# Attention and experts on one core: max scores in the opening, a repacked memory chain, and a longer lead of the maxima

## The reference

```python
q, k, v = qkv of x, 16 heads of 16                      # per batch
attn = softmax(causal(q @ k.T) * scale);  seq_out = attn @ v
w1, w2 = projections of x, previous position / position  # 16 heads of 4
r1, r2 = projections of x
write_lines = exterior(w1, w2); read_lines = exterior(r1, r2)   # 6 components, each divided by its norm
M[t] = decayed sum over s < t of J w[s] (x) J w[s]       # 6 x 6, per head
rd_M = rd @ M;  mem_score = (1 - a) * sum(rd_M * rd) + a * sum(rd_M * rd_M)
gate = sigmoid(memg)
out = (seq_out + mean over heads of (sigmoid(mem_score * mem_scale) * gate) * mem_val) @ out_w.T + out_b
```

## Time and profile before

| | us |
|---|---|
| median of 3 runs | 914.86 (911.75 to 915.72) |
| the profiled execution | 906.65 |
| its span | 904.9 |

### The profile page before, as it was taken

One profiled execution on the slowest core, in us unless ns is written; L12 is line 12 of the kernel. 1 busy time (PEld: TensorE's weight loads), 2 busy tenths in 40 slices (PEclk: granted clock), 3 DMA queues, 4 the chain that ended last, 5 costly groups with the idle time before them and its releaser, 6 DMA issues.

```text
span 904.9 us, 12625 instructions
## 1 busy us (share of the span) xinstructions
PE 763.1 (84%) x4116; PEld 521.5 (58%) x4116; DVE 623.1 (69%) x2123; ACT 353.3 (39%) x709; POOL 409.7 (45%) x334
## 2 busy tenths in 40 slices
PE   6587664888988989989799895787899999999995
PEld 3343432545654656556556553455788788887874
DVE  2126554866886878868878689973677877777775
ACT  2120422544554544545546452373233332422420
POOL 9100644964654655646445565133324433433420
PEclk9887686989998999999989995578899999999998
DMA  8896368347564564656553732513022023022001
GB/s 290 186 238 116 73 98 136 73 93 147 83 158 92 112 150 68 149 110 108 135 106 72 163 66 43 155 47 93 1 71 94 1 94 94 2 93 93 24 1 47
DMA packets 60423, 89.90 MB, mean 99 GB/s; under 512 B 8235, under 2 KB 37317, under 8 KB 60357
## 3 DMA queue, kind: packets, MB, share of 16 engines
q1 hardware_dynamic: 60356, 89.09, 44.0%
HBM read 54.72 MB, written 33.82 MB: 98 GB/s over the span
## 4 chain that ended last, share of the span: by engine, by line
PE 47%; DVE 25%; DMA 12%; POOL 6%; issue 4%; ACT 3%; SPq 3%; ACTq 0%; POOLq 0%; DVEq 0%
PE ps L1242 19%; DVE ps L466 7%; PE ps L336 7%; PE ps L372 6%; PE ps L325 6%; DMA Q<-MT 6%; DVE Ob L514 5%; PE ps L313 4%; DMA qk_scratch<-HL 2%; PE ps L1208 2%; DMA Wm<-mem_scratch 2%; SPq L677 2%; PE ps L230 1%; ACT X L1228 1%; DVE nmax L466 1%
## 5 line engine op out<-in xcount | busy, mean ns | idle before, releaser
L466 DVE CUSTOM_DVE_ANT_0 ps<-ps,mask 128x256 f32<-128x256 f32 (+3 forms) x512 | 238.4, 510 | 87.0 <-PE ps L313 86.9
L409 ACT ACTIVATE Pr<-ps 128x512 f32<-128x512 f32 (+2 forms) x384 | 189.6, 527 | 152.9 <-PE ps L325 146.6
L325 PE MATMUL ps<-Q,K 98*128 98x256 f32 (+2 forms) x512 | 179.2, 393 | 51.0 <-DMA Q<-MT 40.6
L313 PE MATMUL ps<-K,Q 96*128 96x256 f32 (+2 forms) x512 | 163.5, 365 | 30.0 <-DVE nmax L466 28.8
L652 POOL TENSOR_SCALAR_AFFINE_SELECT Pr<-Pr 128x512 f32<-128x512 f32 x128 | 87.9, 692 | 215.7 <-ACT Pr L409 213.5
L1242 PE MATMUL ps<-ew_hi,XT 128*128 128x512 f32 x512 | 180.7, 415 | 0.0
L325 PEld LDWEIGHTS ps<-Q,K 98*128 98x128 f32 x512 | 97.2, 206 | 136.3 <-ACT Pr L409 54.4
L1368 DVE SCALAR_TENSOR_TENSOR A<-ps,cw,A 128x256 f32<-128x256 f32 x256 | 123.7, 483 | 53.6 <-PE ps L1242 42.0
L313 PEld LDWEIGHTS ps<-K,Q 96*128 96x128 f32 x512 | 105.0, 211 | 50.6 <-DVE nmax L466 42.7
L336 PE MATMUL ps<-Pr,V 128*17 128x512 f32 (+3 forms) x1024 | 107.5, 497 | 8.1 <-POOL Pr L652 8.1
L1242 PEld LDWEIGHTS ps<-ew_hi,XT 128*128 128x128 f32 x512 | 100.8, 197 | 21.4
(11 more groups left out here) (183 smaller groups left out, 1124.4 us busy)
## 6 DMA issues: line engine op xcount, KB each, us to landing
qk_scratch<-HL SPq DMA_DIRECT2D x32, 512.0 KB, 3.2
Q<-qk_scratch SPq DMA_DIRECT2D x96, 128.0 KB, 4.0
K<-qk_scratch SPq DMA_DIRECT2D x96, 128.0 KB, 5.7
Pr<-xT SPq DMA_DIRECT2D x8, 512.0 KB, 9.4
xraw<-xT SPq DMA_DIRECT2D x8, 512.0 KB, 6.2
mem_scratch<-Rl SPq DMA_DIRECT2D x16, 256.0 KB, 5.7
mv_scratch<-MV SPq DMA_DIRECT2D x32, 128.0 KB, 1.7
Wm<-mem_scratch SPq DMA_DIRECT2D x16, 256.0 KB, 10.2
```

The lines of the kernel that those rows point to most:

```text
L313: last = nc.tensor.matmul(o, Q[0:STACK, hh, P * i:P * i + P], K[0:STACK, hh, 0:n], start=True, stop=True)
L325: last = nc.tensor.matmul(o, K[0:STACK + 2, hh, P * kt:P * kt + P], Q[0:STACK + 2, hh, T - n:T], start=True, stop=True)
L409: nc.scalar.activation(probs(g % 2, kt, heads[0], len(heads)), src, ACT.Exp, scale=SCALE).then_inc(s_exp, 1)
L466: last = nc.vector.tensor_tensor_reduce(out=scores, in0=scores, in1=mask[:, T - w:T], scale=1.0, scalar=NEG, op0=ALU.add, op1=ALU.max, acc ...
```

## The change

- `LEAD = 8`: `ahead` uses u+8 instead of u+6, so max scores are 20 units ahead of the exp scores; the turn of the maxima comes at unit 4. After the opening, 8 units of group 1 are issued instead of 6.
- In the opening, each of the steps 4 to 7 is followed by three units of the max scores of group 0 (`scores`). The memory tiles 8 to 15 use two PSUM banks in turn instead of four, since the max scores use the others. The stacks of batch 0 are issued behind projections 3, 4, 5 and 6, and x of batch 1 behind projection 4.
- The loads of Wm are in halves of four batches: the first before the maximum rows of group 0, the second after them. The loads of the read projections are in halves too, in the groups 2 and 3 of batch 0 in SP's program, behind the maximum rows.
- The norms of both kinds of lines are computed on POOL, in five steps each (`norms`); DVE keeps the reciprocals, which lie in groups 0 and 1 of batches 1 and 2.
- The memory chain has 18 slots of one group each, from batch 2 to group 1 of batch 6. Three slots hold two halves: slot 0 outer, slot 1 apply and the next outer, slot 2 its apply. Scans lie in units 6, 8 and 10 of slot 0 and units 0, 2 and 4 of slot 2. POOL's masks are called singly and placed between these steps. The products and sums for the score follow on POOL in groups 2 and 3 of batch 6, and DVE has three score steps, in units 5 to 7 of group 1 in batch 7, instead of thirteen.

```diff
+LEAD = 8
+        def tile_bank(m):
+            return ps[m % 4] if m < 8 else ps[2 + m % 2]
-        def opening(project, memory, fold):
+        def opening(project, memory, fold, scores):
...
                 project(j)
+                scores(3 * (j - 4))
...
-                    pe.wait_ge(s_p1e[m % 2], m // 2 - 1)
+                    pe.wait_ge(s_p1e[m % 2], m // 2 - 1 if m < 8 else m // 2)
...
-            k = g + (1 if u < 6 else 2)
-            return k // NG, k % NG, (u + 6) % UNITS
+            k = g + (1 if u + LEAD < UNITS else 2)
+            return k // NG, k % NG, (u + LEAD) % UNITS
...
-                    if u == 6 and not (last and g == NG - 1):
+                    if u == UNITS - LEAD and not (last and g == NG - 1):
                         pe_turn_max(pe, b + (g + 1) // NG, (g + 1) % NG)
...
-                    if first:
-                        dve_write_norms(dve, UNITS * g + u)
-                    if last:
-                        dve_read_norms(dve, UNITS * g + u)
-                    if scan and (g, u) in SCAN_AT:
-                        dve_scan(dve, b, SCAN_AT.index((g, u)))
-                    if last and 9 <= UNITS * g + u < 22:
-                        dve_score_step(dve, UNITS * g + u - 9)
+                    if b in (1, 2) and g < 2 and u in (4, 10):
+                        dve_inverse(dve, Ob[:, 2, :] if b == 1 else Wm[:, 6, :], 2 * g + u // 10,
+                                    ML_WNORM if b == 1 else ML_RNORM)
+                    if (b, g, u) in SCAN_AT:
+                        dve_scan(dve, SCAN_AT.index((b, g, u)))
+                    if last and g == 1 and 5 <= u < 8:
+                        dve_score_step(dve, u - 5)
...
-        SCAN_AT = [(0, 6), (0, 8), (0, 10), (2, 6), (2, 8), (2, 10)]
+        SCAN_AT = [(2 + n // 4, n % 4, u) for n in range(18) if n % 3 != 1
+                   for u in ((6, 8, 10) if n % 3 == 0 else (0, 2, 4))]
...
+                if first and g >= 2:
+                    sp.wait_ge(s_ml, ML_WRITE)
+                    read_rows(g - 2)
                 if not last:
                     sp_projected(sp, b + 1, 2 * g + 1)
...
-                if g == 0 and first:
-                    sp.wait_ge(s_ml, ML_WRITE)
-                    read_rows()
...
             def project(j):
                 sp_projected(sp, 0, j)
-                if j == 0:
+                if j == 3:
+                    sp.wait_ge(s_cst, 1)
+                if 3 <= j < 7:
+                    sp_stack(sp, 0, j - 3)
+                if j == 4:
                     sp_load_x(sp, 1)
-                if j in (1, 3):
-                    if j == 1:
-                        sp.wait_ge(s_cst, 1)
-                    sp_stack(sp, 0, j - 1)
-                    sp_stack(sp, 0, j)
...
+            for i in range(6):
+                sp.wait_ge(s_p1st[i], 16 * ((NB - i + 5) // 6))
+            mem_rows(0, 0, 8, Wm, range(4))
+            sp_max_rows(sp, 0, 0)
...
+            mem_rows(0, 0, 8, Wm, range(4, NB))
-            mem_rows(0, 0, 8, Wm)
-            sp_max_rows(sp, 0, 0)
...
+            def norms(rows, squares, total, between):
+                step(nc.gpsimd.tensor_tensor(squares, rows[:], rows[:], ALU.mult))
+                masks(*between[0])
+                step(nc.gpsimd.tensor_tensor(squares[:, 0:3], squares[:, 0:3], squares[:, 3:6], ALU.add))
+                masks(*between[1])
+                step(nc.gpsimd.tensor_tensor(total, squares[:, 0], squares[:, 1], ALU.add))
+                step(nc.gpsimd.tensor_tensor(total, total, squares[:, 2], ALU.add))
+                step(nc.gpsimd.tensor_scalar(total, total, 1e-24, 0.0, ALU.max, ALU.add))
...
+            for n in range(18):
+                m, k = group_masks(2 + n // 4, n % 4), n // 3 * 2
+                if n % 3 == 0:
+                    outer(k)
+                    masks(*m)
+                elif n % 3 == 1:
+                    apply(k)
+                    masks(*m[0:2])
+                    outer(k + 1)
+                    masks(*m[2:4])
                 else:
+                    masks(m[0])
+                    apply(k + 1)
+                    masks(*m[1:4])
...
-            pe.wait_ge(s_wr, 4)
-            for u in range(UNITS):
-                pe_max_scores(pe, 0, 0, u)
             pe_turn_max(pe, 0, 0)
-            for u in range(6):
+            for u in range(LEAD):
                 pe_max_scores(pe, 0, 1, u)
```

## The result

The changed kernel takes 834.0 us (median of 4 runs, 829.44 to 835.28) against 915.29 for the kernel before beside it (911.75 to 917.45): ratio 0.910, 95% interval 0.907 to 0.913. The forecast was 856 with a range from 838, so the gain was named right in sign and place and its size missed by 22 us. The profiled execution took 833.96 us, span 832.2. Two executions further down, 1048.8 us of the kernel before (e0, granted clock 0.631) and 842.58 us of e1, were slow ones and are left out of medians and comparisons.

What follows compares the result with a forecast made beforehand. PE was taken as nearly the bound in the middle batches, with waits elsewhere and DVE in batch 7. Terms -13 - 23.5 - 7 + 6 - 21 = -58.5 took 906.65 to 848, plus 8.2 gave 856 us; range 838 to 882.

Steps and rivals of the forecast that it cites:

- The start of batch 0: Opening: three edits on loads, max scores and rows let batch 0 start at 84, -13 us, bounds -4 and -20.
- (a): Opening, SP queue: later stack and xraw loads free ACT's HL store; chain gains 10 us, 6 credited, bounds 0 and 10.
- (b): Opening: group 0's twelve max scores run there beside mostly idle PE and DVE; 9 us leave the path.
- (c): Start of batch 0: maximum rows behind only half of Wm, 9 us per half; landing about 82 to 84.
- Rival (1): Opening: the queue stays the bound, only (b) and part of (c) is left; about 868 us, chance 0.15.
- Batches 2 to 6: Middle stage: scans +3.2 and -4.8, triples 0 to 3 each, x splits +6, reciprocals +1.9; +6 us, bounds -6 and +25.
- The lead: Max scores 20 units ahead: counted at nothing, since rows stand behind HL's store on SP; helps in batch 7.
- Batch 7: 25.5 us leave DVE, which stops being the bound; first two groups 28 instead of 48; -21 us, bounds -8 and -28.
- (2): Rival: batch 7 finds new waits in the weights and inputs of the expert phase; 869 us, chance 0.13.
- (3): Rival: packed slots too tight in batches 2 to 6, 4 us a triple, +24; 880 us, chance 0.12.
- (4): Rival: the lead removes the Q<-MT wait and its low clock in six batches, 4.7 each; 828 us, chance 0.06.
- (5): Rival: POOL paces all attention, masks late for PE in every group, 3 us a group, +84; 940 us, chance 0.04.

Runs made afterwards that it cites:

- e0: The kernel before, run again with no edit: 915.5 us, ratio 1.0008.
- e1: C with LEAD = 6 instead of 8, so max scores 18 units ahead: 834.1 us, ratio 0.911.
- e2: C with the stacks of batch 0 back behind projections 1 and 3 and x of batch 1 behind projection 0: 847.67 us, ratio 0.926.
- e4: C with the twelve max scores of group 0 issued behind the opening again, before the turn of the maxima: 830.91 us, ratio 0.9075.
- C: The changed kernel itself, with the whole change and no further edit: 834.0 us, ratio 0.910 to the kernel before.
- e3: C with all eight loads into Wm issued ahead of the first maximum rows: 844.29 us, ratio 0.923.
- e9: e6 with LEAD = 6, the store of HL still ahead of the maximum rows: 827.79 us, ratio 0.9062.
- e13: e12 with LEAD = 6, so the turn of the maxima at unit 6 again: 832.14 us, ratio 0.9062.
- e6: C with POOL waiting for DVE's split of x before the apply at the start of batches 3 and 6: 823.54 us, ratio 0.900.
- e12: e6 with the maximum rows issued ahead of the first store of the projection in every group on SP: 821.9 us, ratio 0.897.
- e7: C with 32 more products of two SBUF operands on DVE in units 1 to 16 of batch 7: 851.8 us, ratio 0.930.
- e10: e6 with group 0's maximum rows ahead of the first 1 MB of Wm and POOL's first two masks before its Wm wait: 829.09 us, ratio 0.904.
- e5: C with the second 2 MB of Wm in one piece ahead of group 3's maximum rows in batch 0: 844.79 us, ratio 0.921.

## Why the prediction was wrong in size

Two steps failed, one of 7 us and one of 8; the result lies 4 us below the lower end of the range.

**The start of batch 0: -13 us forecast, -19.9 measured, because (a) was credited 6 us.** The step "ACT's store lets go at 28 to 31" was right (27.03). The discount behind it, that the loads' bytes come back among the tile stores, was not: DMA rose to 93% busy, and the first load of Wm went out at 63.38, 15.1 us earlier than before, where the forecast had it at 71. From there to PE's first exp score the forecast had 13 us and 13.6 were measured. So the 7 us by which batch 0 starts earlier than forecast are all in the issue of that load, and e2 shows that the place of the stacks makes it: with them back, it goes out 16.6 us later and batch 0 starts 14.5 us later. **(b)** was said to take 9 us off the path, and e4 measures nothing; the scores run under the transfer of the first 1 MB. In the forecast's own working the rows' issue at 73 rests on it, but its landing at 82 to 84 is what the first half of Wm gives anyway, so the error cost little. **(c)** was put at 9 us per half. From the first load to PE's first exp score it was 18.4 us before and 13.6 in C, 4.7 less; e3 gives 6.5 for the second 1 MB, and as much again because eight loads must wait for the later tile stores. Rival (1), the queue as bound of the opening, had it the wrong way round: it left (b) and a part of (c), and it is (a) and (c) that count. Whether the rows land with the first half of Wm or a little before it, which the prediction left open, none of these runs separates.

**The sum's last step.** The stage lengths were worked out from the profiled execution (906.65), and the 8.2 us up to the median were added at the end as if the changed kernel would have the same gap. It hasn't: the profiled execution of C (833.96) lies on its own median, and that of e0 (915.5) does too. Without this step the forecast is 848, 14 above. That doesn't make 8.2 us a mere slip of adding, since the quick execution was also the source of the terms. Against the profile of e0, cut at the same places, C is shorter by 23.0 us in the opening, 24.6 in batch 0, 6.9 in batch 1, 5.0 in batches 2 to 6, and 22.1 from batch 7 to the experts, 81.6 together. By that reckoning nearly the whole miss lies in two terms, the opening (-13 forecast) and the middle (+6 forecast). With one profile of C and two of the kernel before, how the 22 us divide between the last step and the middle stage can't be told more closely.

**Batch 0: right.** 58 forecast, 56.2 measured, and the reason (the order in SP's queue) stands by experiment. **Batch 1: right**, 58 against 57.3; its terms weren't tested one by one.

**Batches 2 to 6: near, but with other terms.** The split of x was said to cost 3 us in each of batches 3 and 6, 6 together; with the wait that orders it the stage is 6.2 shorter. The size was right, the way wasn't: the instruction itself lost only 1.4 us (2.63 instead of 1.21, and the forecast wanted to see 3 or more), the rest is PE's wait and its lower clock behind it. A group with scans costs 1.0 to 1.1, not 1.6. What the forecast held for unchanged is the waits for the rows: before the third groups of batches 2 to 6 they fell from 13.2 to 4.4 us. The same stage of the kernel before took 296.3 and 303.4 in its two profiles, so +6, +2.1 or -5.0 are all within one kernel's scatter. (The sum of a triple of slots on POOL, 29.6 us, is 30.3 by its own terms; nothing hangs on it.) The Trainium skill, SBUF — State Buffer, section SBUF: two separate sides, was read narrowly: on DVE's side a 2-port mode or two SBUF inputs ask for the shared ports, so scores from PSUM aren't held up by POOL. In C, DVE's maxima beside POOL's 6.80 us product take what they take elsewhere, so the trace agrees:

```profile
464.63 6.80 POOL L874 TENSOR_TENSOR Jl<-Rl,Wm 128x3066 f32<-128x3066 f32 x1
```

```profile
465.07 0.46 DVE L468 CUSTOM_DVE_ANT_0 ps<-ps,mask 128x256 f32<-128x256 f32 x1
```

**The lead: nothing forecast, nothing measured in C**, but the reason was wrong in part. PE does wait less for the rows by it, behind the store of HL too: 4.4 us of waits before the third groups against 9.3 in e1. The time doesn't follow, and what takes the gain away isn't shown. That e9 and e13 are slower than e6 and e12 wasn't in the forecast, except that the lead helps in batch 7, where no store of HL is ahead; that is where 2 to 3 us of it are seen.

**Batch 7: right.** 28 forecast for the first two groups, 28.2 measured, DVE at 76% of them instead of the "under 60%" that was to show it. DVE's load was the bound, as the 47.3 us of e7 show. The rest took 36.6, not 37.8.

**The rivals and the signs.** (1) is told above. (2) and (3) didn't come: PE met no new wait in batch 7 above 2.1 us, and no scan waited for POOL. (4) gave 828, the nearest number. Half of its mechanism is there: from 16.4 to 4.4 us the waits before the third groups did shrink. Its price of 4.7 us a batch isn't: batches 2 to 6 didn't get 4.7 us shorter each, and with `LEAD = 6` the time is the same. That its number is near is luck. (5) is out by the 1.7 us. Of the signs, the first exp scores at 84 and 142 came at 77.0 and 133.2, one wait for the rows is over 5 us, the 9.52 at the start of batch 0, and the waits of up to 3.4 us from batch 1 on are fewer and shorter than expected.

## What to carry to other kernels

Take stage lengths from more than one profile, and put the gap between a profiled execution and the median into the range instead of adding it as a term: two profiles of the same kernel differ here by 8.9 us, 7.1 of it in one stage. Before taking work off the path ahead of a transfer, ask whether the transfer that follows is waiting for that work or for bytes queued ahead of it; here a later place for four stacks of loads and one of x was worth 13.7 us and the earlier place of twelve score units nothing. An instruction that stretches by 1.4 us can cost 3 to 4 when the engine behind it is the bound, so read what it releases, and try one wait that orders the two.

## What the runs showed of the hardware

- Two instructions on DVE and POOL that work from SBUF hold each other up in both directions: 2.63 instead of 1.21 us for DVE's, 4.29 instead of 3.48 for POOL's next. That POOL pays too was not expected. Letting DVE go first delayed POOL by 1.8 us there and shortened the two groups by 3.8 and 3.0 us.
- Maximum rows, two DMAs of 8 KB, were seen by PE 6.3 us after issue when the first of 1 MB of loads had gone out 8.1 us earlier (e4) and 6.5 with no load of Wm ahead (e10), and 9.3 to 13.3 when it had gone out some 2 us earlier (C, e2 and eight more). Behind the loads of 2 MB, the first of them 4 to 7 us earlier, it was 16.5 to 19.0 (e3, e5, and the third group of the kernel before), but 11.4 at the start of batch 0 in the kernel before. Over all of C the median from issue to landing is 2.9 us.
- After a wait of 2.30 us, PE's pair of projections took 1.22 us instead of 0.73, in 8 us with a mean granted clock of 0.73; with a wait of 0.89 us there it was 1.00.
- Eleven executions of the kernel before on one chip lie within 13 us, and the two profiled ones differ by 8.9, of which 7.1 lie in stretches where the granted clock was 0.93 instead of 0.96.
